# One core, attention and routed experts: the value product's four parts put together late in a slot, gamma and beta spread out once for all experts

## The reference

```python
x = x + attn(layernorm(x), W_qkv, W_out)
#   softmax(q k^T / sqrt(8) + causal mask) v; heads reshaped, times W_out summed over its heads
x = x + ffn(layernorm(x), ...)
#   probs = softmax(x Wr + br); top 2, weights normalised to sum 1; out = sum of c[t, e] * y_e[t]
def _expert_ffn(xf, Wi_e, bi_e, Wg_e, bg_e, Wo_e, bo_e, g_e, b_e):
    h = gelu(xf @ Wi_e + bi_e) * sigmoid(xf @ Wg_e + bg_e)
    r = xf + (h @ Wo_e + bo_e)
    return (r - mean(r)) * rsqrt(var(r) + 1e-12) * g_e + b_e      # F = 512, D = 128
```

## Time and profile before

| what | us |
|---|---|
| median of 3 runs | 1237.73 |
| lowest and highest | 1237.67, 1241.8 |
| profiled execution, time | 1241.94 |
| its span | 1240.2 |
| PE busy in the span | 1105.6 (89%) |
| DVE busy | 982.0 (79%) |
| ACT busy | 796.9 (64%) |
| POOL busy | 741.8 (60%) |

### The profile page before, as it was taken

One profiled execution on the slowest core, in us unless ns is written; L12 is line 12 of the kernel. 1 busy time (PEld: TensorE's weight loads), 2 busy tenths in 40 slices (PEclk: granted clock), 3 DMA queues, 4 the chain that ended last, 5 costly groups with the idle time before them and its releaser, 6 DMA issues. The chain is left out here.

```text
span 1240.2 us, 27505 instructions
## 1 busy us (share of the span) xinstructions
PE 1105.6 (89%) x8654; PEld 835.8 (67%) x8654; DVE 982.0 (79%) x2792; ACT 796.9 (64%) x1800; POOL 741.8 (60%) x1359
## 2 busy tenths in 40 slices
...
GB/s 145 94 77 113 168 135 166 130 93 125 130 101 125 129 109 123 131 105 113 142 112 93 138 60 36 171 53 53 52 53 54 53 53 53 53 53 53 32 123 305
DMA packets 138270, 127.38 MB, mean 103 GB/s; under 512 B 71848, under 2 KB 96432, under 8 KB 138128
## 3 DMA queue, kind: packets, MB, share of 16 engines
...
## 5 line engine op out<-in xcount | busy, mean ns | idle before, releaser
L808 ACT ACTIVATE probs<-st 128x384 f32<-128x384 f32 (+1 forms) x768 | 389.1, 525 | 204.9 <-PE st L704 181.8
L849 DVE TENSOR_REDUCE neg_max<-sa 128x2 fp32r<-128x1024 f32 (+3 forms) x384 | 395.6, 1036 | 135.1 <-PE sa L689 126.9
L642 POOL TENSOR_SCALAR_AFFINE_SELECT probs<-probs 128x128 f32<-128x128 f32 (+1 forms) x768 | 245.5, 332 | 243.1 <-ACT probs L808 232.6
L704 PE MATMUL st<-q_stack,k_pad 128*128 128x256 f32 (+2 forms) x1024 | 338.4, 372 | 15.6 <-DMA q_stack<-max_scratch 9.1
L684 PE MATMUL sa<-k_pad,q_stack 128*128 128x256 f32 (+2 forms) x1024 | 328.1, 363 | 12.8 <-DVE neg_max L849 6.7
L684 PEld LDWEIGHTS sa<-k_pad,q_stack 128*128 128x128 f32 x1024 | 178.0, 192 | 111.8 <-issue 69.8
L704 PEld LDWEIGHTS st<-q_stack,k_pad 128*128 128x128 f32 x1024 | 177.2, 192 | 48.4 <-ACT probs L808 20.9
L1006 POOL DMA_INDIRECT y_scratch<-z,to_row x142 | 170.7, 1202 | 35.9 <-issue 35.9
L1040 PE MATMUL up<-xt_hi,w_cur 128*128 128x256 f32 x568 | 167.7, 295 | 0.0
L717 PE MATMUL pv<-probs,v_aug 128*32 128x512 f32 (+3 forms) x2048 | 167.1, 445 | 0.0
L1041 PE MATMUL up<-xt_lo,w_cur 128*128 128x256 f32 x568 | 161.6, 285 | 0.0
...
## 6 DMA issues: line engine op xcount, KB each, us to landing
...
k_pad<-k_scratch SPq DMA_DIRECT2D x256, 64.0 KB, 2.5
...
```

The lines of the kernel that those rows point to most:

```text
L642: pool.affine_select(out=blk, in_=blk, compare_op=ALU.is_ge, fill=0.0, base=0, pattern=[[0, w], [1, P]], channel_multiplier=-1).then_inc(m ...
L704: last = nc.tensor.matmul(st[:, t % 2, at:at + w], k_pad[:, G * g + j, kk * P:(kk + 1) * P], q_stack[:, g, S - w:S], start=True, stop=True)
L808: nc.scalar.activation(probs[:, n % 2, j, lo:lo + w], st[:, k % 2, at:at + w], ACT.Exp).then_inc(exp_done, 1)
L849: V.tensor_reduce(neg_max[:, n % 2, heads[0]:heads[-1] + 1, i], scores[:, :, 0:(i + 1) * P], AX.X, ALU.max, negate=True).then_inc(sa_read, 1)
```

## The change

1. In each slot's string PV0 leaves its place behind B1, and PV0 to PV3 stand together behind B8. The side work is laid out anew: V moves from slot 0 to slot 1; Rc from slot 0 to slot 3 of the batch before; in slot 3 Q and K come earlier (Q behind a1, K behind A3), ST stands before A5; Rd, ln2, ln and Rb stand behind a1; Re and Rf, S2 and zn, LGa, Ra and xn, Rc stand directly before PV0.
2. Gamma and beta of all experts are spread out once, in four steps GBa to GBd of `LAST` (two matmuls each and a copy by ACT) into a new SBUF tile `gb_sb`. `gamma_beta` and its semaphore go; `scale` and `shift` read `gb_sb` at the expert's offset.
3. In `down` one bias matmul of 256 columns fills both halves of `y_ps`, which becomes one tile, in place of two of 128.

```diff
 SLOT = {
-    0: "SR A0 B0 a0 B1 PV0 A1 B2 a1 B3 mT mE A2 B4 mW a2 B5 Rc A3 V B6 a3 B7 A4 B8 Rd PV1 PV2 PV3 a4 OT CM B9 mR AR XL A5 B10 RC a5 Re B11 ON",
-    1: "SR A0 B0 a0 Rf B1 PV0 A1 B2 out a1 B3 mT mE A2 S0 B4 mW a2 B5 A3 S1 B6 a3 B7 ln2 A4 B8 S2 PV1 PV2 PV3 a4 OT B9 mR rs2 A5 B10 RC a5 B11 ON",
-    2: "SR A0 B0 a0 ln B1 zn PV0 S3 A1 B2 a1 B3 mT mE rs1 A2 B4 mW a2 B5 zT A3 S4 B6 a3 B7 A4 LG B8 xn PV1 PV2 PV3 a4 OT B9 mR A5 B10 RC LGa a5 B11 ON",
-    3: "SR A0 Ra B0 a0 B1 PV0 S5 A1 B2 a1 B3 mT mE A2 EX S6 B4 mW a2 B5 xT A3 Rb S7 B6 a3 B7 Q A4 B8 Ql PV1 PV2 PV3 a4 OT K B9 mR A5 B10 RC a5 B11 Kl ST ON",
+    0: "SR A0 B0 a0 B1 A1 B2 a1 Rd B3 mT mE A2 B4 mW a2 B5 CM A3 B6 a3 B7 A4 B8 Re Rf PV0 PV1 PV2 PV3 a4 OT B9 mR AR XL A5 B10 RC a5 B11 ON",
+    1: "SR A0 B0 out a0 B1 A1 B2 S0 a1 ln2 B3 mT mE A2 S1 B4 mW a2 B5 V A3 rs2 B6 a3 B7 A4 B8 S2 zn PV0 PV1 PV2 PV3 a4 OT B9 mR A5 B10 RC a5 B11 ON",
+    2: "SR A0 B0 zT a0 B1 A1 B2 S3 a1 ln B3 mT mE A2 S4 B4 mW a2 B5 LG A3 rs1 B6 a3 B7 A4 B8 LGa Ra xn PV0 PV1 PV2 PV3 a4 OT B9 mR A5 B10 RC a5 B11 ON",
+    3: "SR A0 B0 EX xT a0 B1 A1 B2 S5 a1 Rb Q B3 mT mE A2 S6 B4 mW a2 Ql B5 A3 K S7 B6 a3 B7 Kl A4 B8 Rc PV0 PV1 PV2 PV3 a4 OT B9 mR ST A5 B10 RC a5 B11 ON",
 }
...
-FIRST = "ln rs1 xn xT Q Ql K Kl ST SR0 SR1 SR2 SR3 V"
+FIRST = "ln rs1 xn xT Q Ql K Kl ST SR0 SR1 SR2 SR3"
...
-LAST = """PD BU AR Rc- Rd- CM- Re- Rf- W0 W1 W2 out ...
+LAST = """PD BU GBa GBb GBc GBd AR Rd- CM- Re- Rf- W0 W1 W2 out ...
...
+gb_sb = sb("gb_sb", [P, E * 2 * D])
...
+elif kind in GB_STEPS:
+    misc_free(pe, kind, n)
+    pe.wait_ge(r_const, made["b_stack, b_sel"])
+    for half in range(2):
+        e = 2 * GB_STEPS.index(kind) + half
+        last = nc.tensor.matmul(misc[:, half * 2 * D:(half + 1) * 2 * D], b_sel[:, e * P:(e + 1) * P],
+                                b_stack[:, D:3 * D], start=True, stop=True)
+    last.then_inc(misc_written, 1)
...
+    nc.scalar.activation(gb_sb[:, i * 4 * D:(i + 1) * 4 * D], misc[:, :], ACT.Copy).then_inc(gb_done, 1)
...
+nc.tensor.matmul(y_ps[:, :, :], b_sel[:, bass.ds(e * P, P)],
+                 b_stack[:, 0:D].unsqueeze(1).broadcast_to([P, 2, D]), start=True, stop=True)
 for h in range(2):
-    nc.tensor.matmul(y_ps[h][:, :], b_sel[:, bass.ds(e * P, P)], b_stack[:, 0:D],
-                     start=True, stop=False)
     for c in range(FC):
-        last = nc.tensor.matmul(y_ps[h][:, :], hid[:, u % 2, c, h * P:(h + 1) * P],
+        last = nc.tensor.matmul(y_ps[:, h, :], hid[:, u % 2, c, h * P:(h + 1) * P],
...
-    dve.wait_ge(gb_written, s + 1)
     for h in range(2):
         last = V.scalar_tensor_tensor(z[:, r, h, :], res[:, r, h, :], mean_var[:, r, h, 0:1],
-                                      gb_ps[:, 0:D], ALU.subtract, ALU.mult)
+                                      gb_sb[:, bass.ds(e * (2 * D), D)], ALU.subtract, ALU.mult)
...
-stages(pe, [(0, up_projections), (0, load_expert), (1, down), (-2, transpose_x), (2, gamma_beta)])
+stages(pe, [(0, up_projections), (0, load_expert), (1, down), (-2, transpose_x)])
```

More of the change, by code:

```diff
@@ L203, in attention_and_routed_experts @@
                     "AR": -1, "out": -1, "ln2": -1, "rs2": -1, "zn": -1, "zT": -1, "LG": -1, "LGa": -1,
-                    "Ra": -1, "EX": -1, "Rb": -1, "Rc": -2, "Rd": -2, "CM": -2, "Re": -2, "Rf": -2, "S": -2}
-        FIRST = "ln rs1 xn xT Q Ql K Kl ST SR0 SR1 SR2 SR3 V"
+                    "Ra": -1, "EX": -1, "Rb": -1, "Rc": -1, "Rd": -2, "CM": -2, "Re": -2, "Rf": -2, "S": -2}
+        FIRST = "ln rs1 xn xT Q Ql K Kl ST SR0 SR1 SR2 SR3"
         ONCE = {-1: "WL8", 1: "SU0", 2: "SU1", 4: "SU2", 5: "SU3", 6: "WL0", 7: "WL1", 8: "WL2", 9: "WL3", 10: "WL4",
                 11: "WL5", 12: "WL6", 13: "WL7"}
-        LAST = """PD BU AR Rc- Rd- CM- Re- Rf- W0 W1 W2 out ln2 S0- rs2 zn S1- W3 W4 W5 W6 zT W7 W8 LG LGa S2- S3- Ra EX
+        LAST = """PD BU GBa GBb GBc GBd AR Rd- CM- Re- Rf- W0 W1 W2 out ln2 S0- rs2 zn S1- W3 W4 W5 W6 zT W7 W8 LG LGa S2- S3- Ra EX
                   S4- S5- Rb Rc Rd CM Re Rf S6- S7- RU S0 S1 S2 S3 S4 S5 S6 S7 TB W9 W10 W11 W12 W13 W14 W15"""
@@ L396, in misc_free @@
                                "V": (vaug_done, b_ + 1), "zT": (zT_done, b_ + 1), "LG": (logits_done, b_ + 1),
-                               "CM": (rank_done, b_ + 1), "BU": (b_up_done, 1)}[before]
+                               "CM": (rank_done, b_ + 1), "BU": (b_up_done, 1),
+                               **{step: (gb_done, i + 1) for i, step in enumerate(GB_STEPS)}}[before]
                 pe.wait_ge(done, count)
@@ L625, in constants @@
                                                             base=0, pattern=[[-1, E], [0, P]], channel_multiplier=1))
+                    made["b_stack, b_sel"] = count["const"]
             for kind, k, n in ORDER:
@@ L812, in _ @@
                 act_sequence(act, kind, k, n)
-                if kind == "W":
+                if kind in GB_STEPS:
+                    i = GB_STEPS.index(kind)
+                    act.wait_ge(misc_written, misc_use(kind, n))
+                    act.wait_ge(pv_written, GROUPS_ALL)
+                    nc.scalar.activation(gb_sb[:, i * 4 * D:(i + 1) * 4 * D], misc[:, :], ACT.Copy).then_inc(gb_done, 1)
+                elif kind == "W":
                     e, m = k // 2, k % 2
@@ L933, in attention_and_routed_experts @@
         up = pb("up", [P, 4, F])
-        y_ps = [pb(f"y_ps{h}", [P, D]) for h in range(2)]
+        y_ps = pb("y_ps", [P, 2, D])
         xt_ps = pb("xt_ps", [P, BR])
-        gb_ps = misc[:, 0:2 * D]
         gathered = [sem(f"gathered{u}") for u in range(NX)]
@@ L1049, in down @@
                     pe.wait_ge(res_done, s)
+                nc.tensor.matmul(y_ps[:, :, :], b_sel[:, bass.ds(e * P, P)],
+                                 b_stack[:, 0:D].unsqueeze(1).broadcast_to([P, 2, D]), start=True, stop=True)
                 for h in range(2):
[L1051 to L1052 removed]
                     for c in range(FC):
[L1054 removed]
+                        last = nc.tensor.matmul(y_ps[:, h, :], hid[:, u % 2, c, h * P:(h + 1) * P],
                                                 wo_sb[:, bass.ds(e * (FC * D) + c * D, D)],
[L1056 removed]
+                                                start=False, stop=True, skip_group_check=True)
                 last.then_inc(y_written, 1)
[L1059 to L1066 removed]
+            stages(pe, [(0, up_projections), (0, load_expert), (1, down), (-2, transpose_x)])
         @block.scalar
@@ L1141, in residual @@
                 for h in range(2):
-                    last = V.scalar_tensor_tensor(res[:, u % NR, h, :], y_ps[h][:, :], 0.5, xg[:, u, h, 0:D],
+                    last = V.scalar_tensor_tensor(res[:, u % NR, h, :], y_ps[:, h, :], 0.5, xg[:, u, h, 0:D],
                                                   ALU.mult, ALU.add)
```

19 lines of the change are left out of this document (7 added, 12 removed).

## The result

| what | before | after |
|---|---|---|
| median of 4 runs, us | 1237.70 | 1264.83 |
| lowest and highest | 1237.27, 1241.8 | 1261.69, 1266.44 |
| profiled execution, time | 1241.94 | 1261.69 |
| its span | 1240.2 | 1259.9 |
| PE busy | 1105.6 | 1077.7 (86%) |

The ratio is 1.0213, with a 95% interval from 1.0188 to 1.0237: 27 us slower, where 8 had been forecast. What follows accounts for the 19.7. The medians of the kernel before that were taken beside the later kernels are 0.7 to 3.7 us above the 1237.70 of this table, so a part of the 27 can be the scatter of before's own median.

A forecast was written before the change was run, and what follows sets the result against it. DVE's chain was taken to bound attention slots, PE the expert blocks: +23.5 us for 13 full batches, -15.5 for the experts, so +8 on 1237.7, 1246 us. Range 1212 to 1266; the forecast's own 1243 to 1253.

The forecast's parts named there:

- rival 3: Slots 3: K's 1.6 us stall lets the granted clock fall; +26 us, 1272, if in each of 13; chance 0.15.
- The merge: Value product: saves PE 0.43 us a slot, adds 0.86 to DVE's bare chain; alone brings nothing where DVE bounds.
- Slots 0 to 2: Attention slots of 11.3, 11.65 and 11.5 us, with Rd, ln2 and ln in front of a2.
- The bare chain of 9.20: The 10.96 us slot from 430.42 less Re and Rf (1.76); becomes 10.06 us with the merge.
- Slot 3: Last slot of a batch: 10.06 + 0.88 (Rb) + 2.2 (K's chain) = 13.1 us.
- K's chain: Slot 3 on PE before A4: K waits for Ql, then K, B6, a3, B7 follow; 2.2 us.
- First batches: First and last batches cancel: 0, bounds -3 and +3; the 13 full batches get +1.8 us each.
- Slot 1 before: Slot 1 of the kernel before: bound by DVE, so removing B0's wait for the row maxima brings nothing.
- The experts: Expert blocks, bound by PE: 0.22 us less in each of 71, to 4.98 us; -15.5 us, bounds 13 and 17.
- Rival 4: Experts: DVE's SBUF reads contend with POOL, beyond 0.09 us for each of four operations; 1273 us; chance 0.03.
- Rival 1: Attention: PE bounds it and side work hides under it; 61 slots gain 0.43 us; 1196 us; chance 0.12.
- Rival 2: Attention: side work in front of a2 costs about half; 1202 to 1231 us, middle 1222; chance 0.15.

The follow-up runs named there:

- the two probes: Changed kernel with a 128x512 memset (485 ns) on DVE added in every slot: in front of mE 1306.73 us, behind a3 1264.4 us.
- the run with K back: Changed kernel with K, Kl and ST of slot 3 at their places of before: 1255.53 us, ratio 1.0123.
- the one-token edit: Kernel with the experts' part and the slots of before (1226.39 us), SR moved behind mW on SP in slot 0: 1217.97 us.
- the run with K late: Changed kernel with slot 3's K behind B8 and Kl behind OT, ST still behind mR: 1254.15 us, ratio 1.0117.

## Why the prediction was wrong in its size

The sign, the experts' gain and the stall in slot 3 came as forecast; +27 us came in place of +8. 1264.83 lies inside the whole range (1212 to 1266), but in the part that was kept for rival 3, whose fall of the clock in the slots 3 is not what put it there: that is luck.

**The merge: right.** It brings nothing where DVE bounds the slot, and puts 0.86 us on the path (measured 0.83 in slot 2, with nothing else moved). That it is 0.86 in every slot is not shown: the others changed by -0.19 (slot 0), +1.69 (slot 1 without waits) and +0.20 (slot 3). The Trainium skill (TensorEngine Tiling (Array Packing), section Tiling Modes) would have had the merge gain one drain a slot; the runs don't show that the drain is absent, only that PE's gain is not on the path.

**Slots 0 to 2: right.** 11.15, 11.47 and 11.58 against 11.3, 11.65 and 11.5. Pieces in front of a2 cost their length; the two probes show the rule with the same instruction in both places (0.38 to 0.57 against 0.0). That all three came within 0.2 is in part luck. The bare chain of 9.20 was read in the slot from 430.42, which holds a wait of B0 for the maxima of 0.43 (432.68, shown above), where slots without it last 10.54 and not 10.96; and Re, counted there at its full 0.80, brought 0.2 to 0.27 when it was taken out.

**Slot 3: mechanism right, size 0.56 short.** K's chain was put at 2.2 and measures 2.52 (13.66 against 11.14 in the run with K back). The prediction named a wait of 0.35 us and left it to the upper bound: K's copy on ACT stands ahead of B6's exponential, and B8 waits for that. After shows B8 0.52 us behind A4 (435.10 to 435.62), where 0.23 to 0.35 is usual in the neighbouring steps; that this is the missing part is read from the trace and was not tested. Two other terms had errors that nearly cancel, which is luck: Rb in front of a2 was put at 0.88 and cost 0.1, as Q's matmuls cover it; the slot without K's chain was put at 10.94 with Rb and is 11.14, so without Rb it would be some 11.0 (an estimate, 11.14 less 0.1) and not 10.06.

**First batches: wrong, and this is the step that failed.** The prediction let the first and last batches cancel (0, bounds -3 and +3) and gave slot 1 of the second batch its regular length. Summed from the OT rows: start -1.1; the first batch's slots +3.9 (slot 3, with K's chain, is 2.4 of them); the second batch +7.7, of which slot 1 is +6.8; then twelve batches +25.4; the last ones -1.1. That is 34.9 where 23.5 were forecast. Of the 11.4 us between, 6 are the second batch beyond a regular one, some 4 the twelve batches (0.32 each, slot 3), and 2 start, first and last. The sentence that `out` moves past masks and costs nothing was written from steady batches; POOL's one-time work stands in the same slot of before (`b_sel` from 110.58 to 115.23, `out` at 116.06), but there ln2 stands behind B7, half a slot later, waits 0.62 us for `out`, and slot 1 took 11.47 us. That `b_sel` in front of `out` makes the long slot is shown by the run with the one-time work moved (18.25 to 11.50); ln2 back at its old place was not tried. Each dependence that is moved forward has to be looked at in the batch where its producer is latest, not in the usual one.

**Slot 1 before: wrong, without effect on the sum.** It was said to be bound by DVE. In nine of 13 full batches it was bound by the arrival of the maxima; its bare length is 10.55. The change removed that wait by moving ST (SR is issued from 2.46 us after the end of slot 3, in before from 5.75) and put ln2 in its place: 11.40 to 11.47. The prediction had the removal of the wait as worth nothing; it was worth 0.6 to 0.85 a batch (11.13 to 10.55 between the two kernels of the one-token edit, 11.40 in before), and the new layout spent it.

**The experts: right.** -15.5 forecast, -15.1 measured. The block is 4.993 us (4.98). The factors' reads, by source in after (ns, min/median/max):

```profile
L1178 DVE SCALAR_TENSOR_TENSOR z<-res,mean_var,gb_sb x142: 336/351/365, 867.6 to 1210.3; 128x128 f32<-128x128 f32 x142
L1187 DVE SCALAR_TENSOR_TENSOR z<-z,inv_dev,gb_sb x142: 340/350/418, 868.3 to 1211.7; 128x128 f32<-128x128 f32 x142
...
L1225 DVE SCALAR_TENSOR_TENSOR x_all<-y,weight,x_all x128: 346/348/352, 1221.7 to 1257.1; 128x128 f32<-128x128 f32 x128
```

They grew from 342 to 351 ns and from 330 (the mean by line in before) to 350, so 2 x 9 + 2 x 20 = 58 ns a block, where 20 had been taken and 380 were free. DVE is busy for 93.16 of 100 us. Rival 4, which needed 90 ns and more for each of the four, didn't come. The like operation of the final addition (L1225) lasts 348 ns, and POOL has no instruction there (the fifth busy time of this stretch):

```profile
1222.00:1257.00 35.00, 0.00 (x0) 0.00 (x0) 34.44 (x127) 0.00 (x0) 0.00 (x0) 0.50 0.93 324
```

These are two different instructions, with a DMA share of 0.19 beside the one and 0.93 beside the other, so that they agree is a hint and no proof that POOL costs nothing; single cases of L1187 reach 418 ns. The rule of the Trainium skill (GPSIMD Engine Reference, section Specifications), that VectorE's instructions with two SBUF inputs contend with POOL, is not borne out by the medians of these rows, nor are they a fair test of it: 54.6 of the 76.6 us of POOL in the steady stretch are indirect DMAs (L1023). Other operations of DVE do vary in the kernel before: the two last ones of ln2 took 234 and 386 ns at 440.32, beside POOL's indirect DMAs, those of ln 170 and 163 ns at 401.20; what stretches them was not tested.

**The other rivals.** Rival 1 falls with the merge alone (1275.72, where 1212 would have been its time without the experts). Rival 2 holds for Rb only. Rival 3 is a mechanism of this kernel, but not at a stall of 1.14 us in the steady slots; in the full batches of after it came once, in the slot of 18.25 us.

**What stays open.** In the run with K late two slots 1 (11.95 and 11.97 us) have neither the wait for the maxima nor that of ln2, and are not explained; nor are the 7 us between the profiled executions and the medians. Whether the changed layout could do with ST at its old place, once SR stands behind mW, was not tried; nor was a layout that joins the short slot 0 of after with the other slots of before.
